# Decoder layer, feed-forward stage: another order of the attention and gate tiles, and the last product of the gate on GpSimd

## What is computed

```
h1 = rmsnorm(x) * ln1 ; h2 = rmsnorm(x) * ln2            # x: 32 x 100 x 256
attn = causal softmax attention, 16 heads of 16, of h1    # Wq, Wk, Wv
attn = attn @ Wo.T
mod  = 0.1 * tanh(attn @ A)
gate = silu(h2 @ W_in.T + mod * (h2 @ A) @ B)             # 1024 wide
up   = h2 @ W_up.T                                        # 1024 wide
out  = layernorm(x + x + (gate * up) @ W_down.T)
```

## Time and profile before

| | us |
|---|---|
| median of 3 runs (3964.13 to 3971.38) | 3969.43 |
| the profiled execution, its own time | 3973.11 |
| its span, first to last instruction | 3971.4 |
| feed-forward's first instruction to the end | 3265 to 3971.4, about 706 |
| a feed-forward group, the same in all eight to 0.1 | 84.55 |
| PE, DVE, ACT, POOL busy in one group | 72.4, 50.7, 29.5, 26.1 |

### The profile page before, as it was taken

One profiled execution on the slowest core, in us unless ns is written; L12 is line 12 of the kernel. 1 busy time (PEld: TensorE's weight loads), 2 busy tenths in 40 slices (PEclk: granted clock), 3 DMA queues, 4 the chain that ended last, 5 costly groups with the idle time before them and its releaser, 6 DMA issues. The chain is left out here.

```text
span 3971.4 us, 94397 instructions
## 1 busy us (share of the span) xinstructions
PE 3606.3 (91%) x34556; PEld 2673.7 (67%) x34556; DVE 2420.2 (61%) x5690; ACT 1700.7 (43%) x2883; POOL 629.0 (16%) x664
## 2 busy tenths in 40 slices
PE   7999999995899999998999999999999968888887
PEld 6989899895566666665666666566666636666666
DVE  4444444445576776766767676676766746665565
ACT  3222232222455554554545555454555534333332
POOL 0000000002111111111101111011111102333222
PEclk9999999997999998999989999898998978988999
DMA  3000000001554646464564646546464521000000
GB/s 98 14 13 12 4 8 12 12 9 41 96 110 85 125 84 120 77 121 88 89 115 81 121 84 106 105 84 119 76 122 87 97 48 41 13 12 12 21 12 13
DMA packets 122425, 257.11 MB, mean 65 GB/s; under 512 B 19140, under 2 KB 99852, under 8 KB 118972
## 3 DMA queue, kind: packets, MB, share of 16 engines
q1 hardware_dynamic: 113744, 244.11, 32.7%
q10 hardware_dynamic: 8300, 7.69, 0.7%
HBM read 99.95 MB, written 9.83 MB: 28 GB/s over the span
## 5 line engine op out<-in xcount | busy, mean ns | idle before, releaser
L1385 DVE CUSTOM_DVE_ANT_0 ca_rowmax<-ca_rowmax,ca_msk 100x420 f32<-100x420 f32 (+1 forms) x1024 | 923.9, 926 | 577.3 <-PE ca_rowmax L1168 572.0
L1109 ACT ACTIVATE ca_prob<-ca_unit 128x800 f32<-128x800 f32 x768 | 640.3, 834 | 466.3 <-PE ca_unit L1292 464.8
L1168 PE MATMUL ca_rowmax<-ca_ks,ca_qs 96*100 96x512 bf16 (+1 forms) x1536 | 535.2, 427 | 92.5 <-DMA ca_ks<-ca_ks 68.0
L1292 PEld LDWEIGHTS ca_unit<-ca_qs,ca_ks 99*128 99x128 bf16 (+1 forms) x6144 | 385.0, 104 | 250.7 <-issue 169.9
L1292 PE MATMUL ca_unit<-ca_qs,ca_ks 99*128 99x100 bf16 (+1 forms) x6144 | 463.2, 220 | 31.1 <-issue 16.4
L1255 PE MATMUL ca_acc<-ca_prob,ca_vaug 128*17 128x100 f32 x12288 | 469.4, 269 | 16.5 <-issue 9.1
L1002 POOL TENSOR_TENSOR ca_key_part<-ca_key_rest,ca_key_part 128x512 bf16<-128x512 f32 (+1 forms) x192 | 209.9, 1100 | 1594.8 <-ACT ca_key_part L1064 1594.8
L1150 PE MATMUL ca_ring<-ca_wvT,ca_ctxT 128*128 128x256 f32 (+1 forms) x1536 | 381.6, 390 | 3.2 <-DVE ca_key_rest L1359 1.6
L1141 PE MATMUL ca_ring<-ca_ctxT,ca_wkT 128*128 128x512 f32 (+1 forms) x768 | 345.9, 573 | 2.4 <-DVE ca_key_rest L1359 2.4
L1168 PEld LDWEIGHTS ca_rowmax<-ca_ks,ca_qs 96*100 96x100 bf16 x1536 | 166.2, 133 | 250.6 <-issue 177.6
L1255 PEld LDWEIGHTS ca_acc<-ca_prob,ca_vaug 128*17 128x17 f32 x12288 | 247.4, 101 | 118.4 <-issue 53.7
(11 more groups left out here) (275 smaller groups left out, 6252.1 us busy)
## 6 DMA issues: line engine op xcount, KB each, us to landing
ca_ks<-ca_key_part SPq DMA_DIRECT2D x768, 90.2 KB, 4.1
ca_ks<-ca_ks SPq DMA_DIRECT2D x64, 722.0 KB, 7.4
ca_ctx<-in_ctx SPq DMA_DIRECT2D x32, 1408.0 KB
ca_ks<-ca_ks SPq DMA_DIRECT2D x64, 361.0 KB, 9.4
ca_msk<-in_mask_BxSxS_ff SPq DMA_DIRECT2D x32, 564.1 KB
sa_w_stage<-in_L_attn_w_qkv SPq DMA_DIRECT2D x12, 512.0 KB, 5.2
sa_x_in<-in_x ACTq DMA_DIRECT2D x8, 400.0 KB
sa_x_res<-in_x SPq DMA_DIRECT2D x8, 400.0 KB
```

The lines of the kernel that those rows point to most:

```text
L1109: act.activation(prob[:, 2 * (p % 2):2 * (p % 2) + 2, :], unit[:, :, 0:QUAD * N], ACT.Exp)\
L1168: last = pe.matmul(rowmax[0:N, s0:s1], qs[0:STACK, par, h, :], ks[0:STACK, par, h, s0:s1], start=True, stop=True)
L1292: return pe.matmul(unit[0:rows(t0 + k), k, j * N:(j + 1) * N], ks[:, par, h, keys(k)], qs[:, par, h, :], start=(j == 0), stop=True, skip_g ...
L1385: dve.tensor_tensor_reduce(rowmax[0:N, s0:s1], rowmax[0:N, s0:s1], msk[:, par, s0:s1], 1.0, -3.0e38, ALU.add, ALU.max, top[:, bank, h:h + ...
```

## The change

It reorders the feed-forward stage and moves one operation.

- The probabilities of unit u are turned in step u+3 and weighted in step u+4 (`TURN = 3`, twelve steps instead of eleven). Within a step PE's order is now s(t), pt0(t-3), the tile between, pt1(t-3), pv(t-4). From step 3 to step 7 pt0 and pt1 lie in the same bank, with up(t) in the other.
- The tile between is up(t) in steps 0 to 7, gate 0, 1, 2 in steps 8, 9, 10 and ua in step 11 (dictionary `between`). Gate 3 follows, then at, gate 4, ta, gate 5, the wait for `w_s`, six closing products, and gates 6 and 7 each with its own.
- Banks are given out by hand: k in 6 and 7, q in 0 and 1, v in 4 and 5, ua in 6, ta in 7, gate f in bank f.
- The next group's inputs are turned between the last gate tile and down (`turn_normed(g + 1)`); ACT and DVE make their high and low parts (`highs`, `lows`) ahead of the residual sums. DVE makes the next group's `normed` in step 9, between the inverse of unit 7 and the copy of `oT` for sequence 2.
- v is copied by ACT instead of DVE. The layer norm's moments are taken right after the sums; its `finish` stands ahead of the units.
- `hid = gated * up` is a POOL instruction; the factor 0.5 goes into ACT's evacuation of up (`scale=0.5`). DVE's `gated` of tile f waits for POOL's `hid` of tile f-2.

```diff
+    TURN = 3
+    STEPS = UNITS + TURN + 1
+    between = {u: ("up", u) for u in range(UNITS)}
+    between |= {UNITS + n: t for n, t in enumerate((("gate", 0), ("gate", 1), ("gate", 2), ("ua",)))}
...
+    fixed = {("xt", 0): 0, ("xt", 1): 1, ("ht", 0): 2, ("ht", 1): 3, ("k", 0): 6, ("k", 1): 7, ("q", 0): 0, ("q", 1): 1,
+             ("v", 0): 4, ("v", 1): 5}
+    place = fixed | {t: 4 + n % 2 for n, t in enumerate(during)} | {("o", b): 6 + b % 2 for b in range(G)}
+    place |= {("at", 0): 4, ("at", 1): 5, ("ua",): 6, ("ta",): 7} | {("gate", f): f for f in range(FC)}
...
+                for f in range(FC):
+                    pool.wait_ge(gated_done, FC * g + f + 1)
+                    pool.tensor_tensor(hid[:, f, :], gated[:, f % 2, :], up[:, f, :], ALU.mult).then_inc(hid_done, 1)
...
+                for step in range(STEPS):
+                    if step < UNITS:
+                        scores_of(g, step)
+                    u = step - TURN
                     if 0 <= u < UNITS:
                         pe.wait_ge(prob_done, UNITS * g + u + 1)
...
+                        turned(g, u, 0)
+                    name, *which = between[step]
+                    if name == "up":
+                        project(g, ("up", step), up_s, hT, step)
+                    elif name == "gate":
+                        gate(g, *which)
+                    else:
+                        ua(g)
                     if 0 <= u < UNITS:
...
+                        turned(g, u, 1)
+                    if u >= 1:
+                        weighted(g, u - 1)
+                gate(g, 3)
...
+                gate(g, 4)
...
+                gate(g, 5)
+                pe.wait_ge(w_done, g + 1)
+                for f in range(6):
+                    gate_end(g, f)
+                for f in (6, 7):
+                    gate(g, f)
+                    gate_end(g, f)
+                if more:
+                    turn_normed(g + 1)
...
+                    if more and step == UNITS + 1:
+                        start(g + 1)
+                    u = step - TURN - 1
                     if 0 <= u < UNITS and u % C == C - 1:
...
+                    if f >= 2:
+
+                        dve.wait_ge(hid_done, FC * g + f - 1)
...
-                    dve.scalar_tensor_tensor(hid[:, f, :], gated[:, f % 2, :], 0.5, up[:, f, :], ALU.mult, ALU.mult)\
-                        .then_inc(hid_done, 1)
+                    dve.sem_inc(gated_done, 1)
```

More of the change, by code:

```diff
@@ L1582, in rows_of, with run_groups @@
             return w.rearrange("(c p) n -> p c n", p=P)
-        def run_groups(eng, group, start, finish=lambda g: None):
-            start(0)
+        def run_groups(eng, group, begin, finish=lambda g: None):
+            begin(0)
             group(0, True, False)
@@ L1708, in square, with highs @@
                 act.activation(squares[:], x[:, b, :], ACT.Square, accum_out=ssq[:, b:b + 1]).then_inc(squared, 1)
[L1710 to L1716, removed]
+            def highs(g):
                 for name, dst in (("xt", xT), ("ht", hT)):
@@ L1722, in group, with begin @@
                             .then_inc(act_highs, 1)
-                if not before:
-                    high_parts(FIRST, len(halves))
-                    act.activation(b_s[:], b_w[:], ACT.Copy).then_inc(w_highs, 1)
+            def begin(g):
+                load(g)
+                high_parts(0, FIRST)
+                for b in range(G):
+                    square(g, b)
+                highs(g)
+                high_parts(FIRST, len(halves))
+                act.activation(b_s[:], b_w[:], ACT.Copy).then_inc(w_highs, 1)
+            def group(g, more, before):
                 if more:
+                    if not before:
+                        act.wait_ge(normed_done, 2)
                     load(g + 1)
[L1729 to L1733, removed]
+                for name, dst in (("k", kT), ("q", qT)):
+                    for c in range(C):
+                        evacuate(act, dst[:, c, :], (name, c), g)
+                for n in range(G // 2):
+                    bank = bk.bank(("v", n))
+                    bk.wait_full(act, ("v", n), g)
+                    act.activation(v[:, 2 * n:2 * n + 2, :, :],
+                                   ps[bank][0:N, :].rearrange("p (b h d) -> p b h d", b=2, h=H), ACT.Copy)\
+                        .then_inc(bk.freed[bank], 1)
+                for step in range(STEPS):
                     u = step - 1
@@ L1764, in group @@
                         .then_inc(tanh_done, 1)
-            run_groups(act, group, start)
+                if more:
+                    highs(g + 1)
+            run_groups(act, group, begin)
         @block.tensor
@@ L1810, in group @@
                     last.then_inc(bk.filled[bank], 1)
[L1811 to L1834, removed]
@@ new lines, in gate, with gate_end @@
+            def gate(g, f):
+                if f == 0:
+                    bk.wait_out(pe, ("s", UNITS - 1), g)
+                bk.wait_empty(pe, ("gate", f), g)
+                cols = slice(f * P, (f + 1) * P)
+                split_products(ps[bk.bank(("gate", f))][:, 0:T],
+                               [(in_s[0][:, ci, cols], in_s[1][:, ci, cols], hT[0][:, ci, :], hT[1][:, ci, :])
+                                for ci in range(C)], pe, stop=False)
+            def gate_end(g, f):
+                bank = bk.bank(("gate", f))
+                pe.matmul(ps[bank][:, 0:T], b_s[:, f * P:(f + 1) * P], w_s[:], start=False, stop=True)\
+                    .then_inc(bk.filled[bank], 1)
@@ new lines, in ua, with turned @@
+            def ua(g):
+                bank = bk.bank(("ua",))
+                bk.wait_empty(pe, ("ua",), g)
+                split_products(ps[bank][0:RS, 0:T], [(a_s[0][:, c, :], a_s[1][:, c, :], hT[0][:, c, :], hT[1][:, c, :])
+                                                    for c in range(C)], pe).then_inc(bk.filled[bank], 1)
+            def turned(g, u, half):
+                tile = ("pt", u, half)
+                bank = bk.bank(tile)
+                bk.wait_empty(pe, tile, g)
+                for j in range(QUAD):
+                    last = pe.transpose(ps[bank][0:N, j * N:(j + 1) * N], prob[:, u % 2, half * QUAD + j, :],
+                                        ident[0:N, 0:N])
+                last.then_inc(bk.filled[bank], 1)
@@ new lines, in weighted @@
+            def weighted(g, u):
+                b, c = divmod(u, C)
+                bank = bk.bank(("o", b))
+                if u == 0:
+                    for n in range(G // 2):
+                        bk.wait_out(pe, ("v", n), g)
+                if c == 0:
+                    bk.wait_empty(pe, ("o", b), g)
+                for half in range(2):
+                    bk.wait_out(pe, ("pt", u, half), g)
+                    quad = 2 * c + half
+                    for j in range(QUAD):
+                        last = pe.matmul(ps[bank][32 * j:32 * j + DH, quad * N:(quad + 1) * N],
+                                         v[:, b, quad * QUAD + j, :], probT[:, u % 2, half, j * N:(j + 1) * N],
+                                         start=True, stop=True)
+                last.then_inc(pv_done, 1)
+                if c == C - 1:
+                    pe.sem_inc(bk.filled[bank], 1)
@@ new lines, in group @@
+            def group(g, more, before):
+                for c in range(C):
+                    bk.wait_out(pe, ("xt", c), g)
+                if not before:
+                    pe.wait_ge(w_lows, FIRST)
+                for c in range(C):
+                    project(g, ("k", c), wk_s, xT, c)
+                for c in range(C):
+                    project(g, ("q", c), wq_s, xT, c)
+                values(g)
+                pe.wait_ge(w_lows, len(halves) + 1)
+                for step in range(STEPS):
+                    if step < UNITS:
+                        scores_of(g, step)
+                    u = step - TURN
@@ L1845, in group @@
-                    u = step - 3
-                    if 0 <= u < UNITS:
[L1847 to L1861, removed]
@@ L2004, in group @@
                             .then_inc(bk.freed[bank], 1)
-                if more:
-                    start(g + 1)
-                if before:
-                    finish(g - 1)
                 bk.wait_out(dve, ("ta",), g)
```

125 lines of the change are left out of this document (43 added, 82 removed).

## The result

The changed kernel takes 3919.07 us (median of four runs, 3912.06 to 3920.93) for 3970.4 of the kernel before in the same measurement: ratio 0.9867, 95% interval 0.9847 to 0.9888, 51 us less. The forecast was 3926, its own range 3904 to 3955. The profiled execution has a span of 3915.8 us for 3971.4.

The account below looks back on a forecast made before the run. The order of PE's work, not an engine's total, bounds the kernel. Stages 9.0 + 37.9 + 10.5 + 3.6 + 15.2 = 76.2 us, with half clock 78.9 a group for 84.6, giving 3926 us; own range 3904 to 3955, whole range 3860 to 3962.

Parts of the forecast that it names:

- Inputs and v: Turning the inputs, then k, q and v: both 1.3 us waits go, 11.5 us becomes 9.0.
- s(3): Scores of step 3 wait for DVE to read s(2): start at 7.5 us, a wait of 2.1 for 2.61.
- The loop over ACT: Steps 3 to 7: pt1 waits for ACT's pt0 behind the exponential; 3.3 us a step, not 3.05; 1.8 in step 3.
- ua: Step 11: PE waits 2.3 us for DVE's oT(2), queued behind the next normed; at starts at 37.9 us.
- The clock: Half-clock falls at s(3), costing 1.0 us, and at ua, costing 1.7 us, in each group.
- more than 8 us of half clock in a group: Sign of being wrong: PEclk at 0.5 that long in a group would point to rivals 3 and 4.
- at to w_s: at 5.4 us, gate 4 1.1, then ta to w_s 4.0 with PE waiting 1.6: 10.5 us for 14.7.
- hid: POOL's product at 0.95 us a tile: hid(7) ends at 9.2 us, down waits 0.9 and takes 15.2.
- rival 1: Waits in the units and half clock smaller than forecast: 8.0 us a group more gained, 3862 us; chance 0.20.
- POOL in front of down: Late hid on POOL holds down back: at 1.9 us a tile 3.6 us a group slower, 3998 us; chance 0.06.
- half clock through all steps: Waits in every step keep the half clock through steps 3 to 7: 7.8 us a group lost, 4031 us; chance 0.04.
- Rival 4: Waits only change place, PE idles as much and the second half-clock stretch stays: about 3965 us; chance 0.06.

Follow-up runs that it names:

- e5: Changed kernel with the next group's inputs turned behind down and DVE's low parts behind the residual sums: 3937.7 us, ratio 0.9896, group 82.1 us.
- e2: Changed kernel with ACT evacuating the first half of the turned probabilities (pt0) ahead of the exponential: 3915.9 us, ratio 0.9848, group 77.2 us.
- e7: Changed kernel with PE computing up(2) twice in step 2, ahead of s(3): 3924.5 us, ratio 0.9873, group 78.6 us.
- e1: Changed kernel with DVE copying oT of sequence 2 ahead of the next group's normed in step 9: 3910.7 us, ratio 0.9822, group 75.4 us.
- e3: Changed kernel with hid computed by DVE behind gated instead of by POOL: 3923.3 us, ratio 0.9864, group 78.8 us.
- e9: e8 with DVE making the next group's normed inputs behind all twelve steps instead of in step 9: 3884.3 us, ratio 0.9785, group 72.5 us.
- e8: Changed kernel with the edits of e1 and e2, and gate 2 moved from step 10 behind gate 5: 3885.3 us, ratio 0.9769, group 74.1 us.

## Why the prediction was right

- **Inputs and v**, 9.0 us forecast. k, q and v take 7.4, s(0) follows without a wait, the turning takes 1.5, and k follows down directly. The low parts and v's copy are hidden as said. My terms for DVE ahead of s(0) add up to 7.3 us, not to the 6.6 that I wrote; measured, DVE ends kz, which s(0) needs, 5.8 us behind the start of k and the scaling 7.0, and s(0) comes at 7.4. The step was right; that the turning itself is free (e5) was missed, since I had down start 5.1 us behind the closings with nothing in its way.
- **s(3)** comes 7.4 us behind s(0) (forecast 7.5), with a wait of 1.87 (2.1).
- **The loop over ACT.** pt1 waits 0.7, 0.5 and 0.4 us; e2, with the same half clock, prices it at 0.5 a group. I had put 1.8 on its first pass alone. That pass ran at half clock, so that PE reached pt1 late and waited only 0.69; in e7, with full clock there, it waits 1.53. What the clock took, the wait gave back, as the prediction assumed with its 1.0 for the fall.
- **ua** waits 2.16 us (2.3), for the reason named. This is the term that was best read ahead, and the one that e1 gives back with interest.
- **The clock.** Falls at both places named. The one at ua is 3.4 us long; e2's groups take 75.4 with no stretch and 76.7 to 76.8 with this one alone, so 1.3 to 1.4 (1.4 by e1) for my 1.7. The one at s(3) is 6.8 us in five groups of eight, 3.4 in the others; the groups with the longer one take 1.1 to 1.6 more. The prediction had 3.4 us there, and named more than 8 us of half clock in a group as a sign of being wrong. There are 10.2 in the group shown and in three others. That sign came, and the time held all the same, because the waits that the longer stretch shortened gave part of it back: half of 6.8 is 3.4 us, and the units came out 2.5 above the 37.9, of which 1.4 belong to ua. So the 2.7 us for the two falls is right in part by luck. From s(0) to at the units take 40.4 us; 37.9 and the 2.7 were 40.6.
- **at to w_s** 10.4 (10.5), the closings 3.7 (3.6), PE's wait for w_s 1.39 (1.6).
- **hid.** POOL's product takes 1.05 us alone and comes every 0.99; I took 0.95 from a line through two shapes. down waits 0.28 + 0.32 + 0.32 = 0.92 us for the 0.9 forecast, but this agreement is partly luck: 0.28 of it is gate 4's bank, which I hadn't seen, and the last hid ends 9.8 us behind the first closing product, not 9.2, while down starts at 5.5 and not at 5.1. POOL's row over the whole kernel:

```profile
L1675 POOL TENSOR_TENSOR ff_hid<-ff_gated,ff_up x64: 1023/1048/1069, 3340.6 to 3893.1; 128x400 f32<-128x400 f32 x64
```

  The estimate of 1.14, worked out from the Trainium skill (GPSIMD Engine Reference, Engine selection: about twice as slow as VectorE with two inputs), was too high and mine too low, by about the same; the measured 1.05 is 1.8 times DVE's 0.57. Yet VectorE would have been no better here (e3), since it has the other half of the pair to do.
- **The rivals.** Small waits (rival 1), POOL in front of down (2), half clock through all steps (3) and waits that only change place (4) didn't come. Rival 4's thought holds in part: PE's idle time goes from 12.2 us a group to 8.0, not to nothing. The other part of the gain is the clock: PE is busy for 70.7 us of a group instead of 72.4, at the same work, with 10.2 us of half clock instead of 13.7.
- **The sum.** 5.7 us a group forecast, 6.2 measured; 0.3 of the 0.5 comes from where I started, since the group I had read was a short one (84.6 for a mean of 84.9). In the whole time I forecast 44 us in the stage, and the profiled executions have 47.8 there.

What stays open: what v's copy on ACT and the new banks give by themselves, which no run undoes; what filling the drains is worth without at's wait; and which of PE's waits has to go for the last half-clock stretches of e9, which cost nothing that can be read there (72.0 with and without one).

## What to carry to other kernels

When a wait is taken away by a longer lag, list what each engine does in the steps where the lag is drained: the wait moves to the first thing there that is queued behind somebody else's long work (here DVE's 3.3 us of inputs for the next group, ahead of a 0.5 us copy that frees a bank). Price a moved step by what stands next to it and not by its own length: 1.5 us of turning were free, because a bank held back the next stage anyway, and moving the product to POOL gave nothing, because DVE makes the two products of a tile in 1.09 us by itself, and with the second one on POOL each tile still takes 0.99, since `gated` then waits for `hid`. And judge such a change by the length of its own loop: the whole time of this kernel moves by more than most of the edits tried here.

## What the runs showed of the hardware that I had not expected

- The half clock comes in stretches of 3.4, 6.8 or 10.2 us, and the same code has it in one group and not in the next: e8 and e9 have it in four groups behind the first and not in the other three, at the same length of a group.
- A half-clock stretch has no price of its own. One of 3.4 us cost 1.0 in e7 (at 20), 1.3 to 1.4 in e2 (at ua), and nothing in e8 and e9 (at 15), where PE waits for DVE and POOL in the steps behind it: in e9 0.3, 0.6 and 1.1 us without the stretch, one of 0.7 with it.
- Useless work in a wait costs nothing and keeps the clock up in part: with 1.1 us more of products in e7 the stretch at 15 (6.8 or 3.4 us) is gone, and one of 3.4 us comes 5 us later in six of seven groups. The length of the group stays the same (78.6 for 78.7).
